# Layer 0's slot layer: routing and slot update as one stage instead of two

## The chip, the cores and the metric

The kernel runs on one core of a Trainium2 chip. One launch computes all four layers. The metric is the device time of a whole launch in microseconds (us); before the change it is 1705.67 us, the median of three runs from 1702.41 to 1711.73.

## The reference, cut to what matters

The program is a four-layer transformer-like block over 2048 tokens of 128 features. Only the second half of layer 0 is touched, a "slot" layer with adaptive layer norm ahead of it and a gated residual behind it:

```
ctx    = concat([x, mean of the 64 slots])           # x: normalised, scaled and shifted tokens
h      = gelu(ctx @ w1.T + b1)                       # 64 hidden
logits = (h @ w2.T + b2) / (|tau| + 0.1)             # 64 slots
alpha  = softmax over the top 8 logits, 0 elsewhere  # 2048 x 64
gi     = (alpha.T @ x) / (alpha.sum over tokens + 1e-8)
new    = GRU cell(gi, slots)                         # r, z: sigmoid; n: tanh
out    = alpha @ (new @ wv.T + bv) @ wo.T + bo
x_res += gate * out
```

## The kernel before, in words

Tokens lie on partitions: 16 tiles of 128 tokens. A layer part is a chain of stages; each is a block with one program for each engine, and the next block begins when all engines have left the last one. Inside a block each engine runs its instructions in the written order, and semaphores tie them together. Nothing reorders: what stands in the file is what an engine does.

Layer 0's slot part has two blocks.

**Routing** (`stage_l0_route`). SyncE issues 14 loads of weights ahead of the block. VectorE sets two constants, waits for the six loads `for_route`, scales the slots, and only then starts the norm (`norm.start`, `norm.normalise`). TensorE waits for the scaled slots, makes their mean and its product with `w1`, then transposes the normalised tiles four at a time (`norm.turn`, which begins with six filler products, `keep_busy`), and multiplies each bank of 512 tokens with `w1`. ScalarE applies scale and shift from PSUM, then Gelu. The logits of 8 tiles fill one PSUM bank. VectorE then works on all 16 tiles at once: scale, `max` (8 largest), `match_replace`, the mask, and after ScalarE's 16 exponentials the product with the mask, the sum, the reciprocal and the share `alpha`. TensorE then transposes `alpha` in 16 products and ScalarE copies the four banks into `alphaT`.

**Slot update** (`stage_l0_slots`). TensorE sums `alpha.T @ xn` over the tiles in one run of 16 products and the share sums (one column) in a second run of 16. VectorE forms `gi`; it is transposed, copied, and eight gate products with four bias and two slot terms among them follow in PSUM bank `ps_g`. Behind them stand the modulation products of layer 1 (`mod_matmuls`): four of one column and two of 384 columns. Sigmoid and tanh on ScalarE and five VectorE instructions give the new slots; three small products with copies between them give `out_w` (64 rows and one of the output bias); 16 products with `alphaT` give the output, which VectorE adds to `x_res`, with statistics for the next norm (`tile_stats`).

A float32 product of this kernel stands in the trace as two MATMUL instructions; a transpose as one.

Of the kernel before, what the change touches and what calls it, by code (L numbers as in the profile page):

```python
# [19 lines left out]
ALU = mybir.AluOpType  # L20
# [79 lines left out]
def c4(j):  # L100
    return slice(j * BANK, (j + 1) * BANK)
# [11 lines left out]
def mod_matmuls(pe, g, layer, wmod, ps_cols, ps_rows, done):  # L113
# [4 lines left out]
    for half in range(2):  # L118
        pe.matmul(ps_rows[:, half, 0:384], g.silu_rep[:, layer, :], wmod[:, 384 * half:384 * half + 384], start=True,
                  stop=True).then_inc(done, 1)  # L120


def mod_copies(act, g, layer, ps_cols, ps_rows, done):
# [5 lines left out]
    for half in range(2):  # L129
        act.wait_ge(done, half + 2)  # L130
        copy = act.activation(g.mod_rows[:, layer, 3 * half:3 * half + 3, :],
                              ps_rows[:, half, 0:384].rearrange("p (j f) -> p j f", j=3), ACT.Identity)
    return copy

# [926 lines left out]
def stage_l0_route(nc, loads, g, alpha, alphaT, w):  # L1061

    with Stage(nc, "l0route") as st:
        norm = adaln_norm(st, g, 0, SCALE_B, SHIFT_B)
        hidT = st.sb("hidT", [HID + 1, S])
        b1 = loads["l0_b1"]
        bias1 = st.sb("bias1", [HID, 1])
        w1T = loads["l0_w1T"]
        w2T = loads["l0_w2T"]
        tau = loads["l0_tau"]  # L1070
# [8 lines left out]
        ps_h = st.ps("ps_h", [HID, 4, BANK])  # L1079
        ps_l = st.ps("ps_l", [P, 2, BANK])  # L1080
        ps_m = st.ps("ps_m", [P, BANK])
        slots_ready = st.sem("slots_ready")
        mean_done = st.sem("mean_done")
        mean_copied = st.sem("mean_copied")
        bias_done = st.sem("bias_done")
        bias_ready = st.sem("bias_ready")
        hid_done = st.sem("hid_done")
        hid_ready = st.sem("hid_ready")
        logits_done = st.sem("logits_done")
        left_ready = st.sem("left_ready")  # L1090
        exp_done = st.sem("exp_done")
        alpha_ready = st.sem("alpha_ready")
        ones_row = st.sem("ones_row")
        turned = st.sem("turned")
        chain = st.sem("chain")
        with st.block() as block:

            @block.tensor
            def _(pe):
# [3 lines left out]
                pe.wait_ge(mean_copied, 1)  # L1103
                pe.matmul(ps_m[0:HID, 1:2], w1T[:, 1, :], mean_slot[:], start=True, stop=True).then_inc(bias_done, 1)
                norm.turn(pe, 0, ps_l[:, 0, :])
                for j in range(NC4):
                    if j + 1 < NC4:
                        if j >= 1:
                            norm.turned(pe, j - 1)
                        norm.turn(pe, j + 1, ps_l[:, (j + 1) % 2, :])  # L1110
                    norm.turned(pe, j)
                    pe.matmul(ps_h[:, j, :], w1T[:, 0, :], g.hT[:, c4(j)], start=True,
                              stop=True).then_inc(hid_done, 1)
                for t in range(NT):
                    if t % 4 == 0:
                        pe.wait_ge(hid_ready, t // 4 + 1)
# [2630 lines left out]
```

## Time and profile before

| | us |
|---|---|
| median of 3 runs | 1705.67 |
| profiled execution | 1703.24 |
| its span, first to last instruction | 1701.4 |
| the slot part of layer 0, 669.0 to 745.1 | 76.1 |
| TensorE / VectorE / ScalarE busy in the span | 1246.0 / 1280.4 / 915.7 |

Times in the rows below are counted from the start of the span. A row of the timeline gives start, length in us, engine, line, operation, output<-inputs, shape and count, and in brackets how long the engine stood idle before it and what ended that. PE is TensorE's matmul side, PEld its weight loads, DVE VectorE, ACT ScalarE, POOL GpSimd. PEclk is the granted TensorE clock as a share of 2.4 GHz: 1.00 or 0.50 (1.2 GHz). Instructions merged in a row may overlap, so the time of one is the length over the count.

### The profile page before, as it was taken

How to read it: one execution, taken by the hardware profiler on the slowest of the kernel's cores; microseconds unless marked ns; L12 is line 12 of the kernel's file. 1: busy time of each engine (PE TensorE's matmuls, PEld its weight loads, DVE VectorE, ACT ScalarE, POOL GpSimd, SP SyncE). 2: the span in 40 equal slices, each digit the busy share in tenths (PEclk: the TensorE clock that was granted, in tenths of full speed). 3: DMA queues.
4: the chain of work that ended last, by engine and by line, in shares of the span. 5: the costliest groups of instructions: out<-in, count | busy, mean ns of one | idle time of the engine just before them, and what ended most of it. 6: DMA issues, size and time to landing. Idle time of an engine off the chain costs nothing. (4 is left out here: it accounts for less than half of the span.)

```text
span 1701.4 us, 29334 instructions
## 1 busy us (share of the span) xinstructions
PE 1246.0 (73%) x10392; PEld 620.7 (36%) x10396; DVE 1280.4 (75%) x3517; ACT 915.7 (54%) x1792; POOL 240.3 (14%) x278
## 2 busy tenths in 40 slices
PE   7899999999999996575993574060217989924676
PEld 4122222222222223354972462030115545613345
DVE  6999999999999952456348238989897477478783
ACT  5699999999999995322510122030003575712563
POOL 3000000000000000013410423030004221100223
PEclk9799999999999998676995687575657788965678
DMA  2100001100000000000004440000002711031001
GB/s 74 38 21 21 20 24 28 28 23 21 21 21 23 19 3 16 1 30 1 2 1 190 112 113 10 0 1 1 1 1 59 221 48 41 5 117 50 22 23 32
DMA packets 45509, 62.85 MB, mean 37 GB/s; under 512 B 12881, under 2 KB 34452, under 8 KB 44964
## 3 DMA queue, kind: packets, MB, share of 16 engines
q1 hardware_dynamic: 38723, 49.71, 9.8%
q0 software_dynamic: 5440, 10.67, 2.4%
q8 instruction: 83, 1.36, 0.3%
q10 hardware_dynamic: 1200, 0.59, 0.1%
q14 instruction: 63, 0.52, 0.1%
HBM read 34.10 MB, written 13.63 MB: 28 GB/s over the span
## 5 line engine op out<-in xcount | busy, mean ns | idle before, releaser
L961 DVE TENSOR_REDUCE l0att_half_negmax<-l0att_ps_m 128x1 f32<-128x1024 f32 x480 | 547.2, 1216 | 5.7 <-PE l0att_ps_m L769 5.7
L901 ACT ACTIVATE l0att_probs<-l0att_ps_sv 128x512 f32<-128x512 f32 x960 | 521.4, 595 | 44.9 <-PE l0att_ps_sv L863 33.3
L801 PE MATMUL l0att_ps_sv<-l0att_probs,l_V_aug 128*32 128x256 f32 x4096 | 325.3, 392 | 4.8 <-ACT l0att_pv_sb L885 4.7
L863 PE MATMUL l0att_ps_sv<-l_Q,l_K 51*128 51x512 bf16 x992 | 194.5, 389 | 4.1 <-ACT l0att_probs L909 2.3
L769 PE MATMUL l0att_ps_m<-l_K,l_Q 48*128 48x512 bf16 x960 | 186.0, 385 | 9.3 <-DVE l0att_half_negmax L961 7.1
L801 PEld LDWEIGHTS l0att_ps_sv<-l0att_probs,l_V_aug 128*32 128x32 f32 x4096 | 83.0, 108 | 197.2 <-issue 100.9
L863 PEld LDWEIGHTS l0att_ps_sv<-l_Q,l_K 51*128 51x128 bf16 x992 | 48.0, 93 | 207.6 <-ACT l0att_probs L901 188.1
L494 POOL CAST l0att_nm<-l0att_negmax 128x16 bf16<-128x16 f32 x16 | 3.2, 198 | 496.0 <-DVE l0att_negmax L924 496.0
L2964 ACT ACTIVATE l3loc_probs<-l3loc_ps_s 128x320 f32<-128x320 f32 x128 | 50.3, 436 | 30.5 <-PE l3loc_ps_s L2933 30.1
L2112 DVE SCALAR_TENSOR_TENSOR l2spk_lif_v<-l2spk_U 128x64 f32<-128x64 f32 (+1 forms) x368 | 61.6, 211 | 0.0
L2987 DVE TENSOR_REDUCE l3loc_negmax<-l3loc_ps_m 128x2 f32<-128x320 f32 x128 | 53.9, 484 | 6.5 <-PE l3loc_ps_m L2884 4.6
L2391 PE MATMUL l2spk_ps<-l_X,l2spk_w_terms 128*128 128x512 bf16 x48 | 12.6, 430 | 62.1 <-DVE l_X L2421 62.1
L769 PEld LDWEIGHTS l0att_ps_m<-l_K,l_Q 48*128 48x128 bf16 x960 | 47.1, 95 | 26.4 <-DVE l0att_half_negmax L961 19.0
L2188 PE MATMUL l2mix_ps<-l_mix_l_wrkvo,l2mix_X 128*128 128x128 f32 x32 | 8.3, 441 | 64.0 <-DVE l2mix_X L2263 64.0
L3384 ACT ACTIVATE l3exp_passed<-l3f_experts_l_places,l3exp_neg_rank 128x257 bf16<-128x257 f32 x112 | 46.0, 499 | 0.0
L2015 DVE TENSOR_TENSOR l1exp_y<-l1exp_ps_y,mod_rows 64x512 f32<-64x512 f32 x24 | 16.4, 683 | 36.4 <-PE l1exp_ps_y L1984 36.4
L2411 ACT ACTIVATE l2spk_U<-l2spk_ps,l2spk_half_b 128x512 f32<-128x512 f32 x2 | 2.3, 1126 | 72.3 <-PE l2spk_ps L2391 72.2
L1644 DVE TENSOR_TENSOR l1chunk_T<-l1chunk_T,l1chunk_ps_t 128x512 f32<-128x512 f32 x20 | 13.8, 688 | 36.0 <-PE l1chunk_ps_t L1545 36.0
L2309 ACT ACTIVATE l2hid_half_b<-l_hidden_l_b 128x4 f32<-128x4 f32 x1 | 0.2, 205 | 74.4 <-PEq L2169 74.4
L2109 DVE SCALAR_TENSOR_TENSOR l2spk_U<-l2spk_lif_v,l_X 128x64 f32<-128x64 f32 x212 | 38.3, 226 | 0.4 <-DVE l2spk_lif_mid L2127 0.4
L3342 PE MATMUL l3exp_ps_c<-l3exp_part,l3exp_ones 128*128 128x15 bf16 x56 | 10.7, 191 | 38.0 <-DVE l3exp_part L3491 37.9
L1599 POOL TENSOR_TENSOR l1chunk_C<-l1chunk_A,l_chunks_masks 128x2048 f32<-128x2048 f32 x7 | 31.6, 4521 | 47.4 <-DVE l1chunk_A L1631 26.0
(762 smaller groups left out, 2403.3 us busy)
## 6 DMA issues: line engine op xcount, KB each, us to landing
l_K<-l_kp SPq DMA_DIRECT2D x192, 32.0 KB
l_Q<-l_qp SPq DMA_DIRECT2D x192, 32.0 KB
l1ffn_W<-in_l_expert_w_dram SPq DMA_DIRECT2D x1, 4096.0 KB
l3f_experts_l_w<-in_l_w_dram SPq DMA_DIRECT2D x2, 2048.0 KB
l_sorted_in<-l1ffn_zeros SPq DMA_DIRECT2D x1, 3072.0 KB
l1exp_rows<-l_sorted_in SPq DMA_DIRECT2D x6, 512.0 KB, 4.7
l_sorted_out<-l1exp_y SPq DMA_DIRECT2D x6, 512.0 KB, 4.6
l_Q<-in_local_mask_q_dram POOLq DMA_DIRECT2D x2, 1170.0 KB, 19.1
```

The source lines that it names most:

```text
L769: mm = pe.matmul(dst[:, i * BANK:(i + 1) * BANK], Q[at, h % HEAD_BUFS, c1(t)], K[at, h % HEAD_BUFS, c4(2 * half + i)], start=True, stop=True)
L801: mm = pe.matmul(ps_v[32 * c:32 * c + 32, cols], V_aug[:, kt, h, :], probs[:, kt % 2, c, cols], start=(kt == 0 and part == 0), stop=(kt == ...
L863: pe.matmul(dst, K[at, h % HEAD_BUFS, c1(kt)], Q[at, h % HEAD_BUFS, c4(2 * pair + i)], start=True, stop=True).then_inc(last_scored[i] if l ...
L901: act.activation(probs[:, kt % 2, c, :], ps_s[:, n % 3, :], ACT.Exp).then_inc(expd, 1)
L961: dve.tensor_reduce(half_negmax[:, h % 2, t, half:half + 1], src, AX_X, ALU.max, negate=True).then_inc(m_read, 1)
L1599: pool.tensor_tensor(C[:, l % 2, :, :], A[:], mask(l, NT), ALU.mult).then_inc(c_ready, 1)
L2015: dve.tensor_tensor(y[:, 4 * n:4 * n + 4, :], ps_y[0:GANG, n % 4, :].rearrange("p (k f) -> p k f", k=4), gates, ALU.mult).then_inc(y_gated, 1)
L2109: link.mark(dve.scalar_tensor_tensor(U[:, t, half], before[:, half], 0.5, X[:, t, half], ALU.mult, ALU.add))
L2112: link.mark(dve.scalar_tensor_tensor(v[:, half], U[:, t, half], 1.0, U[:, t, half], ALU.is_lt, ALU.mult))
L2964: act.activation(probs[:, n % 3, 2 * half:2 * half + 2, :].rearrange("p h c -> p (h c)"), ps_s[:, u % SCORE_BUFS, 0:2 * SPAN], ACT.Exp).th ...
L2987: dve.tensor_reduce(negmax[:, 2 * half:2 * half + 2, t], heads2(src[:, 0:2 * SPAN]), AX_X, ALU.max, negate=True).then_inc(m_read, 1)
L3384: ins = act.activation(passed[:, e % 2, t, :], place_row[:], ACT.Sign, bias=neg_rank[:, e, t:t + 1])
```

## The change

The two blocks become one, `stage_l0_slots`. What moves:

- VectorE starts the norm first, normalises 8 tiles, then sets the constants, waits for the loads, scales the slots, and normalises the other 8. ScalarE starts with the square root. TensorE starts with nine filler products that wait for nothing, and makes the slots' mean in two later places.
- The ones row of `hidT` is set on GpSimd, not on VectorE; GpSimd begins it when the slots are scaled, and the ones row of `alphaT` behind it.
- The routing runs in two halves of 8 tiles: `choose(b)` and `share(b)`.
- Between the logits and the weighted sums TensorE transposes the slots and does the six gate products that don't need `gi`, the modulation columns of layer 1 and the first 384-column product.
- The weighted sum and the share sum of a tile follow one another, and the first 8 tiles start when their shares are there. In a PSUM bank that holds several sums only the first product has `start=True`.
- `alpha` is transposed 8 tiles behind the weighted sums and 8 behind the gates; the second 384-column product follows. Two filler products stand behind each of three small products at the end.
- The output bias row is gated ahead of the routing.

```diff
-                pe.wait_ge(slots_ready, 1)
-                pe.matmul(ps_m[:, 0:1], w.slots[:], mean_w[:], start=True, stop=True).then_inc(mean_done, 1)
...
+                keep_busy(pe, g, ps_w[:, 3, :], 3)
+                norm.turn(pe, 0, ps_l[:, 0, :])
+                for j in range(NC4):
...
+                    if j == 1:
+                        mean()
+                    if j == 2:
+                        mean_bias()
...
+                gate(both, one, b_ih[:, both], first=True)
+                gate(both, one, b_hh[:, both])
+                gate(third, one, b_ih[:, third])
+                gate(fourth, one, b_hh[:, third])
+                pe.wait_ge(slots_copied, 1)
+                gate(both, slotsT[:], whh[:, 0:2, :].rearrange("p a b -> p (a b)"))
+                gate(fourth, slotsT[:], whh[:, 2, :], last=True)
+                pe.wait_ge(g.wmod_loaded, 16)
+                pe.wait_ge(logits_read, 2)
+                mod_matmuls(pe, g, 1, g.wmod, ps_w[:, 2, 0:4], ps_l, mod_done, halves=(0,))
+
                 for t in range(NT):
-                    pe.matmul(ps_i[:, 0:P], alpha[:, t, :], g.xn[:, t, :], start=(t == 0), stop=(t == NT - 1))
-                for t in range(NT):
-                    mm = pe.matmul(ps_i[:, P:P + 1], alpha[:, t, :], ones[:, 0:1], start=(t == 0), stop=(t == NT - 1),
+                    if t % 8 == 0:
+                        pe.wait_ge(alpha_ready, t // 8 + 1)
+                    pe.matmul(ps_i[:, 0:P], alpha[:, t, :], g.xn[:, t, :], start=(t == 0), stop=(t == NT - 1),
+                              skip_group_check=True)
+                    mm = pe.matmul(ps_i[:, P:P + 1], alpha[:, t, :], ones[:, 0:1], start=False, stop=(t == NT - 1),
                                    skip_group_check=True)
                 mm.then_inc(raw_done, 1)
-                pe.transpose(ps_t[:, 0:SLOTS], w.slots[:], g.ident[0:SLOTS, 0:SLOTS])
+                turn_alpha(0)
+                turn_alpha(1)
                 pe.wait_ge(gi_ready, 1)
...
+                gate(both, giT[:], wih[:, 0:2, :].rearrange("p a b -> p (a b)"), last=True)
+                gate(third, giT[:], wih[:, 2, :], last=True).then_inc(gates_done, 1)
+                pe.wait_ge(mod_copied, 1)
+                turn_alpha(2)
+                turn_alpha(3)
+                mod_half(pe, g, 1, g.wmod, ps_l, mod_done, 1)
...
+            @block.gpsimd
+            def _(pool):
+                pool.wait_ge(slots_ready, 1)
+                pool.memset(hidT[HID:HID + 1, :], 1.0).then_inc(ones_rows, 1)
+                pool.wait_ge(ones_rows, 1)
+                pool.memset(alphaT[SLOTS:SLOTS + 1, :], 1.0).then_inc(ones_rows, 1)
...
+                def choose(b):
+                    ts = slice(8 * b, 8 * b + 8)
+                    dve.wait_ge(logits_done, b + 1)
+                    dve.tensor_scalar(logits[:, ts, :].rearrange("p t s -> p (t s)"), ps_l[:, b, :], itau[:], None,
+                                      ALU.mult).then_inc(logits_read, 1)
+                    dve.wait_ge(logits_read, b + 1)
+                    for t in range(8 * b, 8 * b + 8):
+                        link.mark(dve.max(top[:, t, :], logits[:, t, :]))
+                    link.wait()
+                    dve.tensor_scalar(negtop[:, ts], top[:, ts, 0], -1.0, None, ALU.mult).then_inc(top_ready, 1)
+                    for t in range(8 * b, 8 * b + 8):
+                        link.mark(dve.match_replace(left[:, t, :], top[:, t, :], logits[:, t, :], -3e38))
+                    link.wait()
+                    link.mark(dve.tensor_tensor(left[:, ts, :], left[:, ts, :], logits[:, ts, :], ALU.is_lt))
+
+                def share(b):
+                    ts = slice(8 * b, 8 * b + 8)
+                    dve.wait_ge(exp_done, 8 * (b + 1))
+                    link(dve.tensor_tensor(alpha[:, ts, :], alpha[:, ts, :], left[:, ts, :], ALU.mult))
+                    link(dve.tensor_reduce(total[:, ts], alpha[:, ts, :], AX_X, ALU.add))
+                    link(dve.reciprocal(total[:, ts], total[:, ts]))
+                    dve.tensor_tensor(alpha[:, ts, :], alpha[:, ts, :], bcast(total[:, ts].unsqueeze(2), P, 8, SLOTS),
+                                      ALU.mult).then_inc(alpha_ready, 1)
+
+                norm.start(dve)
+                norm.normalise(dve, range(2 * NC4))
+                link.mark(dve.memset(mean_w[:], 1.0 / SLOTS))
                 dve.memset(ones[:], 1.0).then_inc(ones_ready, 1)
+                link.wait()
+                dve.wait_ge(for_route.done, for_route.all)
+                dve.tensor_scalar(w_slots[:], w_slots[:], slot_scale[:], None, ALU.mult).then_inc(slots_ready, 1)
+                norm.normalise(dve, range(2 * NC4, NT))
```

Three places where the order of instructions changes. First ScalarE, from the block's start to the Gelu (`norm_std` is the square root of the norm, `hT` the scaled bank, `hidT` the hidden layer). Before:

```order
L1130 ACTIVATE l0route_mean_slot<-l0route_ps_m 128x1
L1132 ACTIVATE l0route_bias<-l0route_ps_m,l0ffn_route_l_b 64x1
L441 ACT_TABLE_LOAD
L441 ACTIVATE l0route_norm_std<-l0route_norm_var 128x16
L445 ACTIVATE hT<-l0route_ps_l,mod_cols 128x512 x4
L1139 ACT_TABLE_LOAD
L1139 ACTIVATE l0route_hidT<-l0route_ps_h,l0route_bias 64x512 x4
```

After:

```order
L451 ACT_TABLE_LOAD
L451 ACTIVATE l0slots_norm_std<-l0slots_norm_var 128x16
L455 ACTIVATE hT<-l0slots_ps_l,mod_cols 128x512 x2
L1271 ACTIVATE l0slots_mean_slot<-l0slots_ps_m 128x1
L455 ACTIVATE hT<-l0slots_ps_l,mod_cols 128x512 x2
L1274 ACTIVATE l0slots_bias<-l0slots_ps_m,l0ffn_route_l_b 64x1
L1278 ACT_TABLE_LOAD
L1278 ACTIVATE l0slots_hidT<-l0slots_ps_w,l0slots_bias 64x512 x4
```

The table load and the root come first; the mean's two copies stand behind the second and the fourth scaled bank.

Second TensorE, from the logits to the gates (`ps_i` and in the new kernel `ps_m` hold the weighted sums, `ps_g` the gates). Before:

```order
L1117 MATMUL l0route_ps_l<-l0ffn_route_l_w2T,l0route_hidT 128x64 x16
L1123 MATMUL l0route_ps_h<-ident_sb,l0ffn_alpha 64x128 x16
...
L1248 MATMUL l0slots_ps_i<-xn,l0ffn_alpha 64x128 x16
L1250 MATMUL l0slots_ps_i<-l0slots_ones,l0ffn_alpha 64x1 x16
L1253 MATMUL l0slots_ps_t<-ident_sb,l0ffn_route_l_slots 128x64
L1255 MATMUL l0slots_ps_t<-ident_sb,l0slots_gi 128x64
L1260 MATMUL l0slots_ps_g<-l0ffn_slots_l_wihT,l0slots_giT 64x256
L1261 MATMUL l0slots_ps_g<-l0ffn_slots_l_bih,l0slots_ones 64x256
```

After (L1174 is the helper `gate`; the pair L1227, L1229 stands 16 times):

```order
L1202 MATMUL l0slots_ps_l<-l0ffn_route_l_w2T,l0slots_hidT 128x64 x16
L1208 MATMUL l0slots_ps_m<-ident_sb,l0ffn_route_l_slots 128x64
L1174 MATMUL l0slots_ps_g<-l0ffn_slots_l_bih,l0slots_ones 64x256
...
L116 MATMUL l0slots_ps_w<-silu,wmod 128x1 x4
L124 MATMUL l0slots_ps_l<-wmod,silu_rep 128x384
L1227 MATMUL l0slots_ps_m<-xn,l0slots_alpha 64x128
L1229 MATMUL l0slots_ps_m<-l0slots_ones,l0slots_alpha 64x1
...
L1179 MATMUL l0slots_ps_w<-ident_sb,l0slots_alpha 64x128 x8
L1235 MATMUL l0slots_ps_m<-ident_sb,l0slots_gi 128x64
L1174 MATMUL l0slots_ps_g<-l0ffn_slots_l_wihT,l0slots_giT 64x256
L1174 MATMUL l0slots_ps_g<-l0ffn_slots_l_wihT,l0slots_giT 64x128
```

No transposes of `alpha` stand ahead of the weighted sums, and only two products stand between `gi` and the sigmoid.

Third VectorE, from the normalised tiles to the first half of the routing in the new kernel; GpSimd's two memsets of 1x2048 begin when the slots (L1333 of the new file, between L1330 and the second L435 here) are scaled:

```order
L435 TENSOR_SCALAR xn<-x_res,l0slots_norm_mv,l0slots_norm_rstd 128x128 x8
L1329 MEMSET l0slots_mean_w 64x1
L1330 MEMSET l0slots_ones 128x64
...
L435 TENSOR_SCALAR xn<-x_res,l0slots_norm_mv,l0slots_norm_rstd 128x128 x8
...
L1342 TENSOR_TENSOR l0slots_out_w<-l0slots_out_w,mod_rows 1x128
L1306 TENSOR_SCALAR l0slots_logits<-l0slots_ps_l,l0slots_itau 128x512
L1310 MAX l0slots_top<-l0slots_logits 128x8 x8
L1312 TENSOR_SCALAR l0slots_negtop<-l0slots_top 128x8
L1314 MATCH_REPLACE l0slots_left<-l0slots_top,l0slots_logits 128x64 x8
```

Before, the 16 tiles were normalised in one run with GpSimd idle, and the largest values were searched for all 16 tiles in one run.

## Rows read from the trace of the kernel before

**Rows 1.** Windows: stretch, us, busy of PE, PEld, DVE, ACT, POOL, then PEclk, DMA.

```profile
669.00:745.10 76.10, 46.03 (x219) 31.88 (x219) 32.29 (x143) 19.48 (x41) 1.80 (x1) 0.61 0.03 9
780.00:908.00 128.00, 102.25 (x812) 93.93 (x810) 57.86 (x174) 37.03 (x75) 37.96 (x11) 0.90 0.01 1
```

**Rows 2.** Timeline, VectorE and ScalarE, 675 to 692 us.

```profile
675.40 0.28 DVE L1161 TENSOR_SCALAR l0ffn_route_l_slots<-l0ffn_route_l_slots,l0ffn_route_l_slot_scale 64x128 f32<-64x128 f32 x1 [2.41 <-DMA l0ffn_route_l_w2T<-in_l_w2T_dram]
679.92 4.20 DVE L425 TENSOR_SCALAR xn<-x_res,l0route_norm_mv,l0route_norm_rstd 128x128 f32<-128x128 f32 x16
689.49 2.40 ACT L1139 ACTIVATE l0route_hidT<-l0route_ps_h,l0route_bias 64x512 f32<-64x512 f32 x4
```

**Rows 3.** Timeline, the start of layer 1's first stage.

```profile
745.19 1.28 ACT L441 ACT_TABLE_LOAD   x1 [11.06 <-PEq L3632]
747.74 2.93 PE L376 MATMUL l1proj_ps_q<-ident_sb 128*128 128x128 f32 x12 [5.19 <-DMA l_project_l_wkvb<-in_l_wkvb_dram]
748.02 3.17 DVE L425 TENSOR_SCALAR xn<-x_res,l1proj_norm_mv,l1proj_norm_rstd 128x128 f32<-128x128 f32 x12
```

**Rows 4.** Timeline: normalising beside GpSimd in layer 2, and GpSimd's memset here.

```profile
1284.21 7.72 DVE L425 TENSOR_SCALAR xn<-x_res,l2ffn_norm_mv,l2ffn_norm_rstd 128x128 f32<-128x128 f32 x16
...
1288.04 1.31 POOL L2516 TENSOR_TENSOR x_res<-x_res,l2ffn_product_l_bias 128x512 f32<-128x512 f32 x1 [0.68 <-DVE xn L425]
...
670.62 1.80 POOL L1152 MEMSET l0ffn_alphaT<- 1x2048 f32 x1 [47.36 <-POOLq L3632]
```

**Rows 5.** Timeline, TensorE, transposes and hidden products.

```profile
680.32 2.27 PE L433 MATMUL l0route_ps_l<-ident_sb,xn 128*128 128x128 f32 x8 [0.52 <-DVE xn L425]
...
682.52 1.97 PE L1112 MATMUL l0route_ps_h<-hT,l0ffn_route_l_w1T 128*64 128x512 f32 x2
```

**Rows 6.** Timeline, VectorE and ScalarE, the routing.

```profile
692.34 0.75 DVE L1171 TENSOR_SCALAR l0route_logits<-l0route_ps_l,l0route_itau 128x512 f32<-128x512 f32 x1 [7.57 <-PE l0route_ps_l L1117]
695.83 2.12 DVE L1175 MAX8 l0route_top<-l0route_logits 128x8 f32<-128x64 f32 x16
701.30 3.93 ACT L1144 ACTIVATE l0ffn_alpha<-l0route_logits,l0route_negtop 128x64 f32<-128x64 f32 x16 [8.11 <-DVE l0route_negtop L1179]
708.13 1.23 DVE L1187 TENSOR_TENSOR l0ffn_alpha<-l0ffn_alpha,l0route_total 128x1024 f32<-128x1024 f32 x1
```

**Rows 7.** Timeline, transposes of alpha and weighted sums.

```profile
709.41 3.62 PE L1123 MATMUL l0route_ps_h<-ident_sb,l0ffn_alpha 128*64 128x128 f32 x16 [14.41 <-DVE l0ffn_alpha L1187]
714.23 3.71 PE L1248 MATMUL l0slots_ps_i<-xn,l0ffn_alpha 128*64 128x128 f32 x32 [1.19 <-DVE l0slots_ones L1296]
717.77 1.98 PE L1250 MATMUL l0slots_ps_i<-l0slots_ones,l0ffn_alpha 128*64 128x1 f32 x32
719.78 0.28 DVE L1299 COPY l0slots_raw<-l0slots_ps_i 64x129 f32<-64x129 f32 x1 [5.61 <-PE l0slots_ps_i L1250]
```

**Rows 8.** Timeline, gates, modulation products and the new slots.

```profile
722.33 1.11 PE L1260 MATMUL l0slots_ps_g<-l0ffn_slots_l_wihT,l0slots_giT 128*64 128x256 f32 x2 [0.58 <-DVE l0slots_giT L1308]
728.97 1.87 PE L116 MATMUL l0slots_ps_o<-silu,wmod 128*128 128x1 f32 x8
729.07 0.38 ACT L1288 ACTIVATE l0slots_rz<-l0slots_ps_g 64x256 f32<-64x256 f32 x1 [13.81 <-PE l0slots_ps_g L1268]
730.69 2.91 PE L119 MATMUL l0slots_ps_o<-wmod,silu_rep 128*128 128x384 f32 x4
733.53 0.35 PE L1273 MATMUL l0slots_ps_t<-ident_sb,l0slots_n 64*128 64x64 f32 x1
```

**Rows 9.** Timeline, the output products and the last statistics.

```profile
736.23 6.32 PE L1281 MATMUL l0slots_ps_o<-l0slots_out_w,l0ffn_alphaT 65*128 65x128 f32 x32 [0.78 <-DVE l0slots_out_w L1325]
...
743.31 0.87 DVE L139 BATCH_NORM_STATS2 stats<-x_res 128x6 f32<-128x128 f32 x4
```

**Rows 10.** Windows of TensorE alone: stretch, us, busy time, PEclk, DMA.

```profile
716.70:720.10 3.40, 3.25 (x45) 1.00 0.00 0
720.10:730.40 10.30, 8.43 (x24) 0.50 0.00 0
```

More of the change, by code:

```diff
@@ L110, with mod_matmuls @@
 COLS = (SHIFT_A, SHIFT_B, SCALE_A, SCALE_B)
[L113 removed]
+def mod_matmuls(pe, g, layer, wmod, ps_cols, ps_rows, done, halves=(0, 1)):
     for n, j in enumerate(COLS):
@@ L117, in mod_matmuls, with mod_half, mod_copies @@
     mm.then_inc(done, 1)
[L118 to L123, printed above, removed]
+    for half in halves:
+        mod_half(pe, g, layer, wmod, ps_rows, done, half)
+def mod_half(pe, g, layer, wmod, ps_rows, done, half):
+    pe.matmul(ps_rows[:, half, 0:384], g.silu_rep[:, layer, :], wmod[:, 384 * half:384 * half + 384], start=True,
+              stop=True).then_inc(done, 1)
+def mod_copies(act, g, layer, ps_cols, ps_rows, done, halves=(0, 1)):
     act.wait_ge(done, 1)
@@ L128, in mod_copies, with mod_half_copy @@
         act.activation(g.mod_cols[:, at + which:at + which + 4:3], ps_cols[:, n:n + 2], ACT.Identity, bias=one)
[L129 to L132, printed above, removed]
-    return copy
+    for half in halves:
+        copy = mod_half_copy(act, g, layer, ps_rows, done, half)
+    return copy
+def mod_half_copy(act, g, layer, ps_rows, done, half):
+    act.wait_ge(done, half + 2)
+    return act.activation(g.mod_rows[:, layer, 3 * half:3 * half + 3, :],
+                          ps_rows[:, half, 0:384].rearrange("p (j f) -> p j f", j=3), ACT.Identity)
 def tile_stats(dve, g, src, tiles):
@@ new lines, in mean_bias, with gate, turn_alpha @@
+                def mean_bias():
+                    pe.wait_ge(mean_copied, 1)
+                    pe.matmul(ps_m[0:HID, 1:2], w1T[:, 1, :], mean_slot[:], start=True, stop=True)\
+                      .then_inc(bias_done, 1)
+                def gate(cols, left_side, right_side, first=False, last=False):
+                    return pe.matmul(ps_g[:, cols], left_side, right_side, start=first, stop=last,
+                                     skip_group_check=True)
+                def turn_alpha(j):
+                    for t in range(4 * j, 4 * j + 4):
+                        mm = pe.transpose(ps_h[:, j, c1(t % 4)], alpha[:, t, :], g.ident[:])
+                    mm.then_inc(alpha_turned, 1)
@@ new lines, in _ @@
+                pe.wait_ge(ones_ready, 1)
+                pe.wait_ge(for_slots.done, for_slots.all)
+                one = ones[0:1, :]
+                both, third, fourth = slice(0, 2 * P), slice(2 * P, 3 * P), slice(3 * P, 4 * P)
+                gate(both, one, b_ih[:, both], first=True)
[4 more added lines that the diff above has]
+                gate(both, slotsT[:], whh[:, 0:2, :].rearrange("p a b -> p (a b)"))
@@ L1298, in _ @@
+                for b in range(2):
+                    choose(b)
+                link.wait()
+                for b in range(2):
+                    share(b)
                 dve.wait_ge(raw_done, 1)
-                link(dve.tensor_copy(raw[:], ps_i[:, 0:P + 1]))
+                link(dve.tensor_copy(raw[:], ps_i))
                 link.mark(dve.tensor_scalar(wsum[:], raw[:, P:P + 1], 1e-8, None, ALU.add))
```

278 lines of the change are left out of this document (116 added, 162 removed).

## The prediction

> **What bounds the kernel now.** I read the windows first, to see how much time is at stake. The slot part of layer 0 lasts 76.1 us of a span of 1701.4 [rows 1]; TensorE is busy for 46.0 of it and VectorE for 32.3, so no engine bounds it: it is a chain in which one engine works and the others wait. The granted clock is 0.61 on the mean. Then the timeline of the stretch, engine by engine, asking at each idle time what ended it. The reader is to see seven links, which the change touches one by one:
>
> A. 670.6 (the block's start, GpSimd's memset in [rows 4]) to the first Gelu at 689.49: VectorE waits 2.41 us for a load, and the first normalised tile comes at 679.92 [rows 2].
> B. Gelu to the first bank of logits, 692.34 [rows 6].
> C. 692.34 to the last share, just before 709.41 [rows 6, 7]: VectorE alone, with 16 exponentials in its middle. 17.0 us.
> D. 709.4 to the weighted sums, read at 719.78 [rows 7]: transposes and copies first (4.8 us to 714.23), then 5.5 us of products. 10.4 us.
> E. 719.78 to the sigmoid at 729.07 [rows 7, 8]: 2.6 us to the first gate product at 722.33, and 6.7 us of gate products. 9.3 us.
> F. 729.07 to the transpose of the new slots at 733.53 [rows 8], which stands behind the modulation products: 4.5 us. From there to the first output product at 736.23 [rows 9]: 2.7 us.
> G. 736.23 to 744.2, the last statistics (743.31 + 0.87) [rows 9]: 8.0 us.
>
> The sum is made against the profiled execution: 1703.24 us, of which 1701.4 are span. The median of the runs is 2.4 us above it, less than their spread.
>
> **A, the front.** The norm no longer waits for the loads. Where a stage starts with it, the block begins at 745.19 and the first normalised tile at 748.02 [rows 3], 2.83 us later. Here that gives 673.45, 6.5 us earlier than 679.92. TensorE's nine filler products are 18 instructions of 0.244 us (2.93 for 12 at half clock, [rows 3]): 4.4 us, until 675.1; they end 0.6 us behind the fourth tile (673.45 + 4 x 0.26), so they cost little. Eight transposes take 2.27 us and one hidden product 1.97 at half clock [rows 5]; at full clock half of that. With full clock from about 676 on I get the last bank of hT at 681.4, the bias copy 0.25, the table load 1.28 [rows 3] and the Gelu at 682.95: 6.5 us gained.
>
> Against that stand GpSimd's two memsets. Each takes 1.80 us [rows 4], and they begin when the slots are scaled, at about 676.2, in the middle of the normalising. In layer 2 the same 16 normalising instructions took 7.72 us beside GpSimd's work, against 4.20 here beside nothing [rows 2, 4]; one of GpSimd's instructions there took 1.31 us, and GpSimd in its turn waited 0.68 us for VectorE. So the two engines alternate. For 3.6 us of memsets I take a delay of 3.4 us for tiles 10 to 15, bounds 0 and 3.6: the row in layer 2 is of an operation that reads, these only write. The last tile is then normalised at 681.7 and not at 678.3. TensorE idles from 678 to 680.7, and its clock probably falls again. Worked on: the Gelu at 685.1 at full clock, 687.0 at half. I take 686.0. **A gives 3.5 us**, bounds 2.5 and 6.5.
>
> That is also the place of a rule. The trace shows VectorE's normalising 3.5 us longer beside GpSimd [rows 4]. The Trainium skill says in SBUF — State Buffer, section "Who interferes with whom", that a VectorE instruction in a two-port mode and one on GpSimd lock each other out for the whole of an instruction; the trace agrees, with 7.72 us for 4.20. By that rule taken to the letter the delay is both memsets, 3.6 us; by the reading that an instruction which only writes does not collide it is nothing, and the kernel ends some 2.5 us earlier than I forecast.
>
> Other waits that are new: ScalarE waits for the mean behind its second bank (the third is queued behind it; some 0.5 us, inside the above). VectorE waits for the eight loads of the slot update and for the bias row's DMA ahead of the routing; SyncE has nothing queued behind that DMA, the loads are in by about 679, the row by about 682, and the logits come at 689 or later. Hidden by 6 us or more.
>
> **B** stays: 2.85 us. I take no gain from a higher clock, so the routing starts at 688.9.
>
> **C, the routing in halves.** An operation on 128x1024 takes 1.23 us, one on 128x512 from PSUM 0.75 [rows 6]; halves cost 0.69 each (near the 0.75, which has PSUM to read), so four operations in two halves cost 0.6 more than before. Eight maxima are 1.06 (half of 2.12) and eight replacements 1.6 (half of the 3.2 between 697.95 and the exponentials at 701.30, less 0.17 for the negated maximum). choose(b) is 0.75 + 1.1 + 0.17 + 1.6 + 0.69 = 4.35, share(b) 3 x 0.69 + 0.3 = 2.35: 13.4 us for both. ScalarE's eight exponentials are 1.97 (half of 3.93); the first half starts when the slots are copied and the exp table is loaded, about 4 us behind the first bank, and both end before VectorE wants them. So the wait for ScalarE (the exponentials and the gap behind them) goes: **17.0 − 13.4 = 3.6 us**, bounds 3.0 and 4.2. The shares are ready at 699.9 and 702.3.
>
> **D, the weighted sums.** The transposes and the block's end leave the path: 4.8 us. TensorE fills the pause with the slots' transpose, six gate products (1.04 us for each of the three wide ones, 0.61 for each narrow one, by starts), the columns (1.87) and one 384-column product (half of 2.91) [rows 8]: about 8.5 us from 691.5, until 700, so they end with the first half of the shares. What decides is the clock. Before, the sums ran at full clock (3.71 + 1.98, less overlap, is 5.5 us for 16 tiles), because 16 transposes had run just ahead. The clock then fell at 720.1 behind a stretch of one-column products and stayed at 0.50 through 8.4 us of busy gate products [rows 10]. The new pause is filled with just these. So I take half clock: 0.23 x 2 for a pair of 128 columns (a transpose is 3.62/16 = 0.23) and 0.12 x 2 for the one-column pair, 0.70 a tile, 11.2 us for 16, from 700.1 to 711.3, against 719.78. At full clock the second half would be done 2.85 us behind the shares, at 705.2. **D goes from 10.4 to 9.0: 1.4 us**, bounds 1.4 and 7.6. This is the widest term, and the one in which most of the gain may be left.
>
> **E, the gates.** From the sums to the sigmoid: eight transposes (1.8) run beside VectorE's chain to gi (1.6, unchanged), then 0.4 for gi's transpose, 0.3 for one copy, and two gate products 1.04 + 0.69: 4.3 us, at full clock 3.4. ScalarE has two copies of 0.6 and a table load of 1.28 between; it is free at 3.8. **9.3 − 4.3 = 5.0 us**, up to 5.8.
>
> **F.** The new slots are ready 2.3 us behind the gates; TensorE now has eight transposes (1.8) and one 384-column product (1.3) ahead: 3.1 us. **1.4 us gained**, bounds 1.2 and 2.2. Then three small products with two fillers behind each. A pair of fillers is 0.98 us at half clock and 0.49 at full; the gaps it fills are 0.3 to 0.5. So 2.3 us at full clock, 4.2 at half; the trace of before had full clock here, gained from the 384-column products. I take 3.2: **0.5 us lost**, bounds 0.4 gained and 1.5 lost.
>
> **G.** If the clock holds, VectorE and not TensorE paces the end (0.69 + 0.87 a quarter against 1.58 at half clock): **0.5 us**, bounds 0 and 0.8.
>
> **Sum:** 3.5 + 3.6 + 1.4 + 5.0 + 1.4 − 0.5 + 0.5 = 14.9 us. 1703.24 − 14.9 = **1688.3 us**. All bounds low: 11.6 us, 1691.6; all high: 27.4 us, 1675.8.
>
> **The rivals.**
> *The clock is high in the sums.* For it: TensorE now has no long pause before them; filler and 384-column products surround them. Against: [rows 10], busy yet 0.50. D would give 7.6 and E 5.8: 21.9 us, 1681.3 us. Chance 0.20.
> *The front gives nothing.* GpSimd's memsets take their full 3.6 us, the clock falls in the hole, the logits run at half clock too, and every filler at the end costs its 0.98: A 2.0, B −1, C 3.0, F −1.5: 9.9 us, 1693.3 us. Chance 0.15.
> *It isn't worth what the links say:* another chain through SyncE's loads or ScalarE's tables ends last, 7 us or less gained, 1697 us or later. Against: each wait in the trace has its releaser among those removed. Chance 0.05.
> *Slower: layer 1 loses its clock.* The 128 us from 780 on have TensorE busy for 102.25 at 0.90 of full clock [rows 1]. If the earlier arrival left these at half clock for more than a quarter of the stretch, 23 us or more, that would turn the gain into a loss; all of it would be some 90 us. A loss of 25 gives 1713. Against: each stage raises its own clock by fillers [rows 3]. Chance 0.03.
> My forecast's case has 0.57.
>
> **How the numbers follow.** Predicted 1688.3. The range 1679 to 1697 takes in the high-clock rival down to 1679 and the poor front with the scatter of the runs; outside lie the last two rivals and the far end of the second. A measurement of this kernel can tell about 0.5%, 8.5 us, from no change. Faster by more than that needs 1697 or less: the first three cases, less a little for scatter, 0.91; within 0.5% 0.06; slower 0.03.
>
> **What would show it.** First normalised tile 2.8 us behind the block's start. Two of the tiles 8 to 15 lasting near 1.8 us beside a memset (if all last 0.35, A is larger). Eight exponentials running under VectorE's second choose. A granted clock of 0.50 through the weighted sums with about 0.35 us for each instruction pair; 1.00 there means the first rival. Sigmoid 4.3 us behind the sums. The forecast is wrong if the part from block start to the last statistics is outside 50 to 66 us (73.6 before), or if what comes behind changes by more than 3 us.

## The result

The new kernel takes 1683.91 us (median of 4 runs, 1682.84 to 1685.66); the kernel before took 1704.09 beside it. The ratio is 0.9878, 95% interval 0.9857 to 0.9900: 20.2 us or 1.2% faster. Forecast were 1688.3 us, in a range of 1679 to 1697. In a second comparison the new kernel took 1684.68 against 1705.36, ratio 0.9893 (0.9862 to 0.9925).

The profiled execution took 1683.57 us, its span 1681.8. The slot part shrank from 76.1 us [rows 1] to 56.8. Windows of the new kernel, columns as in rows 1:

```profile
669.00:725.80 56.80, 43.53 (x237) 34.54 (x237) 34.11 (x148) 19.03 (x42) 3.63 (x2) 0.74 0.05 12
```

TensorE is busy for 2.5 us less with 18 matmul instructions more, at a granted clock of 0.74 for 0.61 on the mean; VectorE is busy for 1.8 us more. No work was saved: what shrank is the waiting. Link by link, in us from the block's start (670.61 before, 670.99 now) to the start of the next block; two profiles of the new kernel:

| link | before | forecast | new | new again |
|---|---|---|---|---|
| A block start to first Gelu | 18.88 | 15.4 | 13.79 | 15.61 |
| B to the first bank of logits | 2.85 | 2.85 | 2.84 | 2.98 |
| C to the last share | 17.02 | 13.4 | 13.36 | 13.35 |
| D to the sums read | 10.42 | 9.0 | 8.20 | 8.21 |
| E to the sigmoid | 9.29 | 4.3 | 3.56 | 4.00 |
| F to the transpose of the new slots | 4.46 | 3.1 | 2.35 | 2.80 |
| F to the first output product | 2.70 | 3.2 | 2.43 | 2.42 |
| G to the next block's start | 8.96 | 8.5 | 8.28 | 8.29 |
| sum | 74.58 | 59.7 | 54.81 | 57.66 |

Timeline of the front, VectorE, GpSimd, ScalarE and one row of TensorE (answers to rows 2 and 4):

```profile
673.82 2.14 DVE L435 TENSOR_SCALAR xn<-x_res,l0slots_norm_mv,l0slots_norm_rstd 128x128 f32<-128x128 f32 x8
...
676.22 4.99 DVE L435 TENSOR_SCALAR xn<-x_res,l0slots_norm_mv,l0slots_norm_rstd 128x128 f32<-128x128 f32 x8
...
676.35 1.80 POOL L1157 MEMSET l0slots_hidT<- 1x2048 f32 x1 [52.72 <-DVE l0ffn_route_l_slots L1333]
...
678.21 1.83 POOL L1159 MEMSET l0slots_alphaT<- 1x2048 f32 x1
...
680.17 0.44 PE L443 MATMUL l0slots_ps_l<-ident_sb,xn 128*128 128x128 f32 x2 [1.39 <-DVE xn L435]
...
684.78 2.40 ACT L1278 ACTIVATE l0slots_hidT<-l0slots_ps_w,l0slots_bias 64x512 f32<-64x512 f32 x4
```

The reader is to see eight of the same instructions take 2.14 us alone and 4.99 beside two memsets, and TensorE waiting for them at the end of it. One by one, the first of the second eight lasts from 676.22 to 678.24 and the first memset to 678.15; another lasts from 678.22 to 680.12 and the second memset to 680.04. The other six have about their usual length. The first tile comes 2.83 us behind the block's start, as in rows 3.

The sums and the gates (answers to rows 7 and 8):

```profile
698.74 0.69 PE L1227 MATMUL l0slots_ps_m<-xn,l0slots_alpha 128*64 128x128 f32 x2 [2.11 <-DVE l0slots_alpha L1324]
...
709.08 1.72 PE L1179 MATMUL l0slots_ps_w<-ident_sb,l0slots_alpha 128*64 128x128 f32 x8
...
709.18 0.28 DVE L1351 COPY l0slots_raw<-l0slots_ps_m 64x129 f32<-64x129 f32 x1 [8.21 <-PE l0slots_ps_m L1229]
...
711.38 0.86 PE L1174 MATMUL l0slots_ps_g<-l0ffn_slots_l_wihT,l0slots_giT 128*64 128x256 f32 x4 [0.32 <-DVE l0slots_giT L1359]
...
711.44 1.28 ACT L1291 ACT_TABLE_LOAD   x1
...
712.74 0.38 ACT L1291 ACTIVATE l0slots_rz<-l0slots_ps_g 64x256 f32<-64x256 f32 x1
```

TensorE stood idle for 2.11 us ahead of the sums and then needed 10.3 us for 16 tiles, 0.64 each. The sigmoid comes directly behind its table load, and the gate products are done 0.5 us before it: in this profile, with the clock full, ScalarE and not TensorE ends link E. The clock over these links, windows of TensorE alone (columns as in rows 10):

```profile
689.90:698.70 8.80, 6.73 (x22) 0.51 0.00 1
...
698.70:709.10 10.40, 10.36 (x65) 0.50 0.00 0
...
710.80:721.40 10.60, 8.99 (x64) 1.00 0.01 2
```

The clock is half through the side products and the sums, as forecast, and full from the transpose of gi (it rose at 710.5) to the last output product.

### The profile page after: what moved, and what is told of

Same layout as the page of the kernel before. It is cut to its first block and busy times, and to the rows that moved or that the text cites. A ratio compares the mean times of both kernels' runs of the same rounds, so it can differ in the third digit from the quotient of the medians.

```text
span 1681.8 us, 29366 instructions
## 1 busy us (share of the span) xinstructions
PE 1244.3 (74%) x10410; PEld 622.9 (37%) x10414; DVE 1283.4 (76%) x3521; ACT 915.2 (54%) x1793; POOL 242.1 (14%) x279
## 5 line engine op out<-in xcount | busy, mean ns | idle before, releaser
L2432 PE MATMUL l2spk_ps<-l_X,l2spk_w_terms 128*128 128x512 bf16 x48 | 13.4, 451 | 61.2 <-DVE l_X L2462 61.2
L2056 DVE TENSOR_TENSOR l1exp_y<-l1exp_ps_y,mod_rows 64x512 f32<-64x512 f32 x24 | 16.4, 683 | 35.6 <-PE l1exp_ps_y L2025 35.6
```

## The experiments

Launches of one kernel scatter by several us (the new kernel, 1680.01 to 1698.75 in six runs), because later stages, unchanged, do. In the two profiles of the new kernel the latent attention of layer 3 took 75.5 and 70.8 us and the stretch at the end 99.1 and 104.1. So effects of 1 to 5 us are read from the links of a profile and the launch times stand beside them. Each link is from one profile of each version. Only e9, e10 and e11 were timed beside the new kernel; the launches of the others can be held against it only by their ratio to the kernel before. "Stage" is from block start to block start: 54.8 and 57.7 for the new kernel.

**e0_new_again.** The new kernel, unchanged.

> The new kernel once more, unchanged, for its own scatter. In the first profile it took 54.8 us from block start to block start, 13.8 of them to the first Gelu. Theory (the stage's time depends on when the clock rises against the block's start): the links behind the routing differ by less than 0.5 us, the front by up to 2 us, and the whole by 20 us against before, within 3. Rival (the profile is exact to 0.2 us in each link).

Stage 57.66, launch 1684.68, 20.7 us below the kernel before. The theory holds: the stage differs by 2.9 us between the two profiles, 1.8 of it in the front and 1.0 in the rest, with no link behind the routing off by more than 0.5. The front's share shows in the windows of TensorE; this one first, then the first profile for the same stretch:

```profile
681.00:686.00 5.00, 5.00 (x13) 0.50 0.00 0
```

```profile
681.00:686.00 5.00, 3.88 (x16) 1.00 0.01 2
```

In both, TensorE idles while VectorE is held up. In one the clock fell behind that idle time, in the other it did not. E and F are longer here for the same reason: the clock rose at 718.4, in the other profile at 710.5.

**e4_old_front.** The front of before in the new kernel.

```diff
-                norm.start(dve)
-                norm.normalise(dve, range(2 * NC4))
...
+                link(dve.memset(hidT[HID:HID + 1, :], 1.0))
...
                 dve.tensor_scalar(w_slots[:], w_slots[:], slot_scale[:], None, ALU.mult).then_inc(slots_ready, 1)
-                norm.normalise(dve, range(2 * NC4, NT))
+                norm.start(dve)
+                norm.normalise(dve, range(NT))
```

(TensorE's mean products and ScalarE's copies ahead of the norm again, no three fillers.)

> The new kernel with the front of before: VectorE sets the constants, waits for the loads and scales the slots ahead of the norm, the mean's products and copies stand first on TensorE and ScalarE, and hidT's row of ones is VectorE's. Theory (the front gained by starting the norm 6.5 us earlier and lost some of it to the memsets): block start to first Gelu is 18.9 us as before the change, against 13.8 to 15.6 in the runs with the new front, and the rest stays; 3.3 to 5.1 us slower. Rival (the fillers made the gain, through the clock): 1 to 2 us slower only, as the first normalised tile is late but TensorE catches up.

A is 19.15 us, all later links within 0.2 us of the new kernel's second profile; stage 61.01, launch 1690.41, ratio to before 0.9920 (0.9904 to 0.9937). The front is worth 3.5 to 5.4 us, by which of the new kernel's two profiles it is held against. The theory holds.

**e1_memsets_late.** GpSimd's rows behind the normalising.

```diff
-                pool.wait_ge(slots_ready, 1)
+                pool.wait_ge(norm.tile_normed, NT)
                 pool.memset(hidT[HID:HID + 1, :], 1.0).then_inc(ones_rows, 1)
```

> The new kernel, but GpSimd sets the two rows of ones only when all 16 tiles are normalised. In the new kernel the second eight normalising instructions took 4.99 us beside the memsets, the first eight 2.14. Theory (VectorE and GpSimd hold each other up): the second eight take 2.1 us again, the first Gelu comes 1.9 us earlier (about 11.9 us behind the block's start instead of 13.8), and the whole kernel is 1.9 us faster than the new one. Rival (TensorE or the loads set the front, the delay is hidden): the normalising is short again but the Gelu moves by less than 0.5 us.

Its timeline:

```profile
677.54 2.14 DVE L435 TENSOR_SCALAR xn<-x_res,l0slots_norm_mv,l0slots_norm_rstd 128x128 f32<-128x128 f32 x8
...
679.94 2.13 DVE L435 TENSOR_SCALAR xn<-x_res,l0slots_norm_mv,l0slots_norm_rstd 128x128 f32<-128x128 f32 x8
...
682.13 1.80 POOL L1157 MEMSET l0slots_hidT<- 1x2048 f32 x1 [56.43 <-DVE xn L435]
```

The second eight take 2.13 us again and A is 11.78: 2.0 us less than the better of the two profiles. TensorE has no long idle time in it, and the clock is full from 680.7 to the logits. Stage 53.21. In the link the theory is confirmed and the rival out. Launch 1679.15, ratio to before 0.9853 (0.9837 to 0.9870); the new kernel has 0.9878 (0.9857 to 0.9900). The way is right, but the intervals overlap, so the 1.9 us are not shown in the launch.

**e2_whole_routing.** All 16 tiles in one routing.

```diff
-                for b in range(2):
-                    choose(b)
+                choose()
                 link.wait()
-                for b in range(2):
-                    share(b)
+                share()
...
```

(`choose` and `share` now work on all 16 tiles in one run, and TensorE and ScalarE wait for all of them. The negated maxima stay ahead of the replacements.)

> The new kernel with the routing for all 16 tiles at once, as before the change; everything else new. Theory (the halves hide ScalarE's exponentials and let the weighted sums start early): from the first bank of logits to the last share 17.0 us instead of 13.4, and the sums 16 x 0.64 = 10.3 us at half clock instead of 8.2 behind the last share: 5.8 us slower than the new kernel. Rival (the halves pay only in the routing, because the sums find a full clock when they run in one piece): 3.7 us slower in the routing and 2.5 us given back in the sums, 1.2 us slower in all.

C is 13.33 us. Neither theory nor rival had that: the halves bring nothing in the routing here. D is 10.49 us, 2.3 more, near the 10.3 of the theory, for the sums can begin only behind the last share. Stage 57.26, launch 1689.43 (seven runs, 1678.58 to 1698.82), ratio to before 0.9923 (0.9899 to 0.9948), too scattered to size the loss. The second bank of logits and ScalarE's exponentials in this kernel:

```profile
688.59 0.75 DVE L1306 TENSOR_SCALAR l0slots_logits<-l0slots_ps_l,l0slots_itau 128x512 f32<-128x512 f32 x1 [1.03 <-PE l0slots_ps_l L1202]
...
691.53 0.17 DVE L1312 TENSOR_SCALAR l0slots_negtop<-l0slots_top 128x16 f32<-128x16 f32 x1
...
691.74 3.93 ACT L1285 ACTIVATE l0slots_alpha<-l0slots_logits,l0slots_negtop 128x64 f32<-128x64 f32 x16 [1.34 <-DVE l0slots_negtop L1312]
...
694.85 1.22 DVE L1316 TENSOR_TENSOR l0slots_left<-l0slots_left,l0slots_logits 128x1024 f32<-128x1024 f32 x1
```

The exponentials start 3.1 us before the mask, where before they started beside it (701.30, [rows 6]). In `choose` the negated maxima stand ahead of the replacements; before they stood behind. That is a second edit in the same lines, which the halves hid from me. It gave the next experiment.

**e8_max_first.** The kernel before, with that order alone.

```diff
+                dve.tensor_scalar(negtop[:], top[:, :, 0], -1.0, None, ALU.mult).then_inc(left_ready, 1)
                 for t in range(NT):
                     link.mark(dve.match_replace(left[:, t, :], top[:, t, :], logits[:, t, :], -3e38))
-                dve.tensor_scalar(negtop[:], top[:, :, 0], -1.0, None, ALU.mult).then_inc(left_ready, 1)
```

> The kernel before the change with one line moved: the negated maxima (and the signal to ScalarE) stand ahead of the 16 replacements instead of behind them. Theory (what the routing gained in the new kernel came from this order, not from the halves): ScalarE's 16 exponentials run beside the replacements, VectorE's wait of 2.9 us for them goes, and from the first bank of logits to the last share it takes 14.1 us instead of 17.0; the kernel is 2.9 us faster than before. Rival (the halves hide them, this order does not): the exponentials still end behind the mask, 16 us or more.

C is 14.03 us, 3.0 less than before: VectorE no longer waits for the exponentials, only for the second bank of logits.

```profile
696.40 0.75 DVE L1171 TENSOR_SCALAR l0route_logits<-l0route_ps_l,l0route_itau 128x512 f32<-128x512 f32 x1 [1.74 <-PE l0route_ps_l L1117]
...
699.56 3.92 ACT L1144 ACTIVATE l0ffn_alpha<-l0route_logits,l0route_negtop 128x64 f32<-128x64 f32 x16 [4.80 <-DVE l0route_negtop L1177]
...
702.66 1.23 DVE L1182 TENSOR_TENSOR l0route_left<-l0route_left,l0route_logits 128x1024 f32<-128x1024 f32 x1
...
703.92 1.22 DVE L1184 TENSOR_TENSOR l0ffn_alpha<-l0ffn_alpha,l0route_left 128x1024 f32<-128x1024 f32 x1
```

That second wait is 1.74 us, and 1.03 in e2: the 0.7 us by which the two differ in C. The 32 instructions of the logits take 4.57 us here, where the clock fell to 0.50 in their midst, and 3.76 at the full clock of e2. The launch did not show the gain: 1703.90 against 1704.00, ratio 0.9989 (0.9973 to 1.0006). In the profile the stage is 72.15 against 74.58. Besides the 3.0 us in C, it gained 1.0 in E, where the first two gate products still ran at full clock, and lost 1.4 at the end, where the clock was half (2.70 to 3.22 and 8.96 to 9.81). So the order is worth 3.0 us in the link, and not shown in the launch.

**e3_gates_behind.** The six gate products behind gi again, of which the diff shows the first.

```diff
-                gate(both, one, b_ih[:, both], first=True)
...
                 pe.wait_ge(gi_copied, 1)
+                gate(both, one, b_ih[:, both], first=True)
...
```

> The new kernel with the six gate products that don't need gi put back behind gi, so only these leave TensorE's pause. Theory (they are worth their time at the clock that holds behind gi, which was 1.00 in the new kernel): three wide of 0.52 and three narrow of 0.31 us, 2.5 us more between the sums and the sigmoid, 2.5 us slower. Rival (without them in the pause the clock is half behind gi as it was before the change): 5 us slower or more.

E is 8.02 us against 3.56 and 4.00: 4.0 to 4.5 us, at half clock throughout. That is between the 2.5 of the theory and the 5 of the rival, and nearer the rival: the clock did not rise until 722. Stage 61.32, launch 1686.31, ratio 0.9901 (0.9884 to 0.9919).

**e5_turn_first.** All transposes of alpha ahead of the sums.

```diff
+                for j in range(NC4):
+                    if j % 2 == 0:
+                        pe.wait_ge(alpha_ready, j // 2 + 1)
+                    if j == 2:
+                        pe.wait_ge(mod_copied, 1)
+                    turn_alpha(j)
                 for t in range(NT):
-                    if t % 8 == 0:
-                        pe.wait_ge(alpha_ready, t // 8 + 1)
...
-                turn_alpha(0)
-                turn_alpha(1)
...
```

(The other two transposes leave their place behind the gates, and ScalarE's four copies of `alphaT` all stand ahead of the sigmoid's table load.)

> The new kernel with all 16 transposes of the shares ahead of the weighted sums, eight behind each half of the shares (before the change they stood there too). Theory (what decides the sums is the granted clock, and full transposes raise it): the transposes end about 1.8 us behind the last share, the sums then run in 5.5 us at full clock, so the sums are read 7.5 us behind the last share instead of 8.2, and with the shorter tail behind the gates it is 0 to 1.5 us faster than the new kernel. Rival (the clock stays at half through the sums): the sums end 12.1 us behind the last share, 4 us slower than the new kernel.

D 7.15 and E 3.10, against 8.20 and 3.56: 1.5 us. Stage 55.33 with the slow front (A 15.53) in it, launch 1682.40 (0.9848 to 0.9892 of before). A tile's four products take 0.34 us here, not 0.64. The clock rose at 705.5, among the last transposes. The theory is confirmed: with more work on the path, at the other clock, the path is shorter. The 0.46 us in E come from ScalarE's copies, which are out of the way.

**e6_fill_8** and **e10_fill_4.** Eight, or four, filler products ahead of the sums.

```diff
                 mod_matmuls(pe, g, 1, g.wmod, ps_w[:, 2, 0:4], ps_l, mod_done, halves=(0,))
+                keep_busy(pe, g, ps_l[:, 1, :], 8)
```

> The new kernel with eight filler products (16 instructions of 128 columns) behind the first 384-column product, in TensorE's pause ahead of the weighted sums. Theory (the sums wait for nothing but the clock): the fillers last 3.9 us at half clock and end 1.8 us behind the first half of the shares, the clock rises, the sums take 0.34 us a tile instead of 0.64 and are read about 5 us behind the last share instead of 8.2: 3 us faster. Rival (the fillers come too late or too few for the clock): the sums start 1.8 us later at half clock, 1.8 us slower.

> Four filler products instead of eight ahead of the weighted sums. Theory (it takes an unbroken run of full products for the clock to rise, longer than these 2 us): they cost nothing, as they fit the pause of 2.1 us, but the sums stay at half clock and are read 8.2 us behind the last share. Rival (the pause is the only thing that kept the clock down): full clock, 3.3 us.

With eight: D 3.32, E 3.10, stage 50.39. With four: D 3.73, E 3.10, stage 51.91. The theory of the first holds in its way and came out larger, 4.9 us in D for 3: the clock rose among the fillers, and they ended with the first half of the shares. Of the second the rival holds: the clock was full with four. TensorE with four fillers, and the clock of the window behind them:

```profile
699.10 1.63 PE L124 MATMUL l0slots_ps_l<-wmod,silu_rep 128*128 128x384 f32 x2
700.52 1.79 PE L386 MATMUL l0slots_ps_l<-ident_sb 128*128 128x128 f32 x8
702.25 0.43 PE L1228 MATMUL l0slots_ps_m<-xn,l0slots_alpha 128*64 128x128 f32 x2
```

```profile
702.00:706.00 4.00, 4.00 (x48) 0.99 0.00 0
```

The 384-column product and the fillers are 3.1 us of wide products without a gap, and the sums find a full clock. The fillers both close the pause and are wide; products of one column in the same pause were not tried. But a pause is not needed for half clock: the sums of the new kernel stayed at 0.50 through 10.4 us without one. The launch of the kernel with eight was 1686.85 (1680.93 to 1687.30), ratio to before 0.9887 (0.9866 to 0.9908), no faster than the new kernel, though its stage is 4.4 us shorter; with four, one run took 1677.84.

**e7_no_end_fill.** Without the six fillers at the end, taken out in this way at three places.

```diff
-                keep_busy(pe, g, ps_l[:, 0, :], 2)
```

> The new kernel without the six filler products between the three small products and ahead of the output products. Theory (they hold the clock): the three small products take 2.3 to 2.4 us as now, but the clock falls by the output products, which then pace the end: 9.0 us from the first output product to the next block's start instead of 8.3, 0.7 us slower. Rival (the clock holds without them, or falls at the same place): within 0.2 us of the new kernel.

The small products take 2.40 us, as with fillers, so these cost nothing. G is 8.64, 0.35 more. The clock fell within the output products:

```profile
717.00:723.00 6.00, 5.16 (x31) 0.73 0.01 3
```

The theory's direction is right and its size half, in one profile of each. (F took 3.02 and E 4.00 in it, ahead of any change: half clock, as in e0.) Launch 1685.97, ratio to before 0.9890 (0.9866 to 0.9914), not to be told from the new kernel.

**e11_whole_fill_12.** Whole routing and twelve fillers.

> The routing for all 16 tiles at once, with twelve filler products ahead of the sums. Theory (the halves pay only in the sums, by what TensorE can do before the last share): 13.3 us from first logits to last share as with halves; at full clock the sums are read 5.7 us behind it, against 3.3 with halves: the halves are worth 2.4 us. Rival (with the clock at full the halves are worth nothing): 3.3 to 4 us.

C 13.32, D 5.64: theory confirmed. Against 3.32 the halves are worth 2.3 us at full clock too, and all of it in the sums. Stage 51.76, one run, 1686.40.

**e9_late_and_fill.** The late memsets and the eight fillers together.

> The new kernel with two additions: GpSimd sets its rows behind the normalising, and eight filler products stand ahead of the weighted sums. Theory (the two gains add up): front 11.8 to 13.5 us, last share to sums read 3.3 us, block start to block start 47.5 to 49.5 us against 54.8, and the launch 5 to 7 us faster than the new kernel of this call. Rival (what the stage gains, the stages behind it give back, as the launch times of the kernel with eight fillers hint: 4.4 us less in the stage, no less in the launch): launch within 2 us of the new kernel.

A 11.77 and E 3.10, but D 6.21, 2.9 us more than with the eight fillers alone. The fillers and the first of the sums, in this profile:

```profile
696.68 3.62 PE L386 MATMUL l0slots_ps_l<-ident_sb 128*128 128x128 f32 x16
...
700.23 0.60 PE L1228 MATMUL l0slots_ps_m<-xn,l0slots_alpha 128*64 128x128 f32 x2
```

In e6 they took 2.71 us and ended as the first half of the shares came; here they ran at half clock to their end, and the sums began 2.8 us behind that half, which was ready at 697.46. So eight fillers are free only where the clock rises among them. Stage 50.34, above the theory's range. Launch 1680.92 against 1684.68 for the new kernel in the same comparison, 3.8 us less; ratio to before 0.9856 (0.9835 to 0.9878), where the new kernel has 0.9893 (0.9862 to 0.9925). That is less than the 5 to 7 us of the theory and more than the 2 of the rival. The two intervals overlap, so against the new kernel in the launch its gain is likely and not shown. The stage is as short as in e6 (50.39), no shorter.

## Why the prediction was right

The sum was 14.9 us; the profiles gave 19.8 and 16.9, the launches 20.2. The direction and the kind of gain were right: waits went, and no work. Each term came out within its bounds, and nearly all above the value taken for it. But C came out for another reason than the one given, so there the number was luck, and F was missed in its second part.

- **A**, 3.5 forecast, 5.1 and 3.3 measured. The first tile came 2.83 us behind the start, exactly as forecast. The hold-up of VectorE by GpSimd was forecast at 3.4 us and came at 2.8 (4.99 against 2.14); e1 shows that it is the memsets. So an operation that only writes does it, which the rows of before had left open: of the forecast's two bounds, 0 and 3.6, the upper is near. The sign named for it, two tiles of near 1.8 us, came as 2.02 and 1.90. The forecast took the mean of two clocks, 14.5 us at full and 16.4 at half, and both occur: 13.79 and 15.61, each 0.7 lower.
- **C**, 3.6 forecast, 3.7 measured, for the wrong reason. The term is headed "the routing in halves", and "So the wait for ScalarE ... goes" credits them. e2 has 13.33 without halves, and e8 has 14.03 in the old kernel with one line moved: 3.0 us are the order, and the other 0.7, between e8 and e2, is a shorter wait for the second bank of logits. The sum of VectorE's durations was right, which is why the number was. With the negated maxima early and the logits at full clock the halves are worth nothing in C: they hide a wait of 1.03 us, and their shorter operations cost about as much more. Where the clock falls among the logits, as in e8 with its wait of 1.74, they may be worth some 0.7; no run has halves beside such a clock.
- **D**, 1.4 forecast, 2.2 measured. The clock was half, as argued from [rows 10]: windows at 0.50. A tile took 0.64 us and not the 0.70 I had from a pair of transposes and a pair of one-column products, and 16 times that difference is nearly all of the 0.8 us by which D was better. The sums began 2.24 us ahead of the last share, forecast 2.2. The side products did not end with the first half of the shares, as forecast, but 2.11 us earlier, a pause that the forecast did not have and that e6 and e10 fill. That this term had most of the gain left in it was right: e6 takes 4.9 us more from it.
- **E**, 5.0 forecast, 5.7 and 5.3 measured; 5.0 was for half clock. The clock rose at 710.5 in the first profile, behind the first transposes, and stayed half through this link in the second. ScalarE's table load ends the link at 3.56 in the first (the forecast had ScalarE free at 3.8); only with the copies earlier (e5) or the sums at full clock (e6) is it 3.1.
- **F**, a gain of 1.4 less a loss of 0.5 forecast, gains of 2.1 and 0.3 measured, 1.7 and 0.3 again. Together they are off by 1.5 and 1.0 us, the second part with the other sign, though within its bound of 0.4 gained: "So 2.3 us at full clock, 4.2 at half ... I take 3.2". In both profiles the clock was full before the fillers came (from 710.5, and from 718.4, among the transposes and the 384-column product ahead of them), and at full clock the fillers fit into the gaps; e7 has the same 2.4 us without them.
- **G**, 0.5 forecast, 0.7 measured; VectorE paces it at full clock. e7, without the fillers, has 0.35 less of it.

Of the rivals, the high clock in the sums did not happen by itself and had to be made. The poor front did not happen in the size given; its clock did fall in one of the two profiles. (Its sum, with the forecast's other terms, is 10.8 us and 1692.4, not the 9.9 and 1693.3 written; both lie in the range.) Layer 1 kept its clock: the same stretch of it, counted from its block's start, is 760.6 to 888.6 now, with a granted clock of 0.89 and TensorE busy for 103.98 us, against 0.90 and 102.25 [rows 1]. All that stands behind the stage took 956.0 us in the new profile and 956.2 before.

What stays open is why the launch times of e6 and e8 don't show what their stages show. The stages behind, which no edit touched, took 956.0 and 952.7 us in the two profiles of the new kernel, and from 949.4 to 961.4 in those of its variants. Three of the four with fillers ahead of the sums are at the long end (961.4 in e6, 959.6 in e9, 961.4 in e11), and the fourth is not (952.0 in e10). That would fit the rival of e9, by which later stages give the gain back, and it would fit chance; with one profile of each, no run here separates them. Open too is why the clock fell in one front and not in the other: the two profiles have the same instructions, and it was not varied on purpose.

## What to carry to other kernels

In a chain of small steps, read which engine waits, and then look at what stands in the queue ahead of the instruction that it waits for: one VectorE line behind 16 others cost 3 us. Where TensorE stands before a run of small products, look at what runs just ahead of them: four wide products that nobody needs, in a pause, took the needed ones from 0.64 to 0.34 us a tile. Keep them short enough for the pause, or they stand on the path themselves, as in e9. And two edits in the same lines need two experiments; a sum that comes out can hide that the wrong one was credited.

## What the runs showed of the hardware

- A GpSimd memset of one partition, 1.80 us, holds up VectorE's float32 instructions with one input and one output in SBUF: eight took 4.99 us beside two memsets instead of 2.14. Two of the eight took nearly all of it, 2.02 and 1.90 us, each until a memset had ended. The memsets were not slower (1.80 and 1.83).
- The same sums ran at either clock, by what stood ahead of them. Through 10.4 us of unbroken pairs of 128-column and one-column products (busy 10.36) the granted clock stayed 0.50; with 3.1 us of wide products ahead (e10) the same products ran at 0.99, 0.34 us a tile for 0.64.
- One kernel's stage varied by 2.9 us between two profiles of the same instructions, by where the clock rose and fell.
